# A wait on the run-sum fourteen visits back before every second gather of a graph kernel

## The reference

```python
def _L0_gnn_ref(x, W, M, edge_src, edge_dst):
    self_term = x @ W
    msg = x @ M
    agg = jax.ops.segment_sum(msg[edge_src], edge_dst, num_segments=x.shape[0])
    return jax.nn.relu(self_term + agg)
...
x = x + _L0_gnn_ref(_layernorm(x, axis=-1), L0_gnn_W, L0_gnn_M, src, dst)
x = x + _L0_ffn_ref(_layernorm(x, axis=-1)[None], ...)[0]
```

## Time and profile before

| | |
|---|---|
| median of 3 runs | 4304.4 us |
| their range | 4269.7 to 4313.66 us |
| profiled execution, first to last instruction | 4291.8 us |
| first gather of the first graph to the start of its last run-sum | 63.7 to 2811.1 us |
| median gather of the visits | 946 ns |

### The profile page before, as it was taken

One profiled execution on the slowest core, in us unless ns is written; L12 is line 12 of the kernel. 1 busy time (PEld: TensorE's weight loads), 2 busy tenths in 40 slices (PEclk: granted clock), 3 DMA queues, 4 the chain that ended last, 5 costly groups with the idle time before them and its releaser, 6 DMA issues. The chain is left out here.

```text
span 4291.8 us, 43359 instructions
## 1 busy us (share of the span) xinstructions
PE 2685.8 (63%) x13459; PEld 2000.5 (47%) x13459; DVE 2156.3 (50%) x5820; ACT 902.7 (21%) x1563; POOL 2161.1 (50%) x2248
## 2 busy tenths in 40 slices
PE   2465766676665676766777766761197555556754
PEld 1343544454443444554555544541196444445653
DVE  5676666666644444544444444420045444445666
ACT  3001111111122222111111111110054333334433
POOL 4565665556554565554555555557502434343121
PEclk9667988887887888888888888885598777777877
DMA  9575665655555565555555655540131111111146
GB/s 288 168 239 170 199 186 160 189 170 184 176 175 157 176 186 168 163 184 165 181 183 174 186 182 183 186 97 11 13 105 33 32 35 33 25 43 34 43 129 191
DMA packets 476804, 601.22 MB, mean 140 GB/s; under 512 B 72486, under 2 KB 415390, under 8 KB 474526
## 3 DMA queue, kind: packets, MB, share of 16 engines
q1 hardware_dynamic: 378766, 375.94, 26.7%
q0 software_dynamic: 97216, 219.88, 18.9%
q10 hardware_dynamic: 592, 2.64, 0.2%
HBM read 313.06 MB, written 286.79 MB: 140 GB/s over the span
## 5 line engine op out<-in xcount | busy, mean ns | idle before, releaser
L1700 POOL DMA_INDIRECT ring<-xn_d,srci x1611 | 1564.8, 971 | 1165.6 <-issue 453.7
L1504 PE MATMUL wide<-ring,one_hot 128*128 128x256 f32 x3222 | 984.0, 441 | 631.1 <-DVE ring L817 460.0
L817 DVE SCALAR_TENSOR_TENSOR ring<-ring,same_v,wide 128x256 f32<-128x256 f32 x1610 | 769.8, 478 | 1193.4 <-remote 662.5
L1504 PEld LDWEIGHTS wide<-ring,one_hot 128*128 128x128 f32 x3222 | 665.9, 218 | 900.3 <-issue 489.9
L1610 PE MATMUL wide<-tab_parts,low_hot 128*128 128x208 bf16 x6288 | 656.5, 261 | 334.1 <-issue 312.7
L1734 POOL DMA_INDIRECT g<-tab_d,srt x500 | 479.1, 958 | 633.3 <-DMA sum_d<-g 484.3
L1610 PEld LDWEIGHTS wide<-tab_parts,low_hot 128*128 128x128 bf16 x6288 | 575.6, 100 | 415.2 <-issue 380.3
L1562 PE MATMUL wide<-w2s,hh 128*128 128x256 f32 x1568 | 428.1, 422 | 149.6 <-issue 89.4
L1552 PE MATMUL wide<-xt,w1s 128*128 128x512 f32 (+1 forms) x832 | 423.4, 637 | 41.5 <-ACT hh L1237 39.4
L1237 ACT ACTIVATE hh<-wide,b1c 128x512 f32<-128x512 f32 (+1 forms) x208 | 137.7, 662 | 1469.0 <-remote 584.8
L1562 PEld LDWEIGHTS wide<-w2s,hh 128*128 128x128 f32 x1568 | 337.9, 217 | 225.7 <-issue 103.3
(11 more groups left out here) (369 smaller groups left out, 1740.9 us busy)
## 6 DMA issues: line engine op xcount, KB each, us to landing
run_d<-ring SPq DMA_DIRECT2D x201, 1024.0 KB
ring<-xn_d,srci POOLq DMA_INDIRECT x1611
y_d<-yo SPq DMA_DIRECT2D x196, 128.0 KB
comb<-y_d SPq DMA_DIRECT2D x28, 896.0 KB, 10.5
low_row<-low_d SPq DMA_DIRECT2D x13, 1024.0 KB
sum_d<-g SPq DMA_DIRECT2D x15, 768.0 KB, 3.4
g<-tab_d,srt POOLq DMA_INDIRECT x500
xn_d<-ring SPq DMA_DIRECT2D x7, 896.0 KB, 6.9
```

The lines of the kernel that those rows point to most:

```text
L817: dve_at["run", j] = step(V.scalar_tensor_tensor(out=o, in0=ring[:, (j - 1) // JC % RING, (j - 1) % JC, :], scalar=same_v[:, j:j + 1], in1 ...
L1504: T.matmul(wide[:, 4 + j // 2 % 2, j % 2 * D:(j % 2 + 1) * D], one_hot[:, j // 4 % 4, j % 4, :], ring[:, j // JC % RING, j % JC, :], start ...
L1700: G.indirect_dma_start(out=ring[:, s, j % JC, :], out_offset=None, in_=xn_d, in_offset=at_rows(srci[:, j:j + 1])).then_inc(sem(f"gather{s} ...
```

## The change

Before every gather of an even visit from the fourteenth on, GpSimd waits until VectorE has made the run-sum of the visit fourteen places back. The new constant shifts the line numbers by one up to the place of the wait, and by three behind it.

```diff
@@ -28,6 +28,7 @@
 LATE = 2
 EARLY_STARTS = 27
+LEAD = 14
 
@@ -1697,6 +1698,8 @@
                 G.wait_ge(dve_step, dve_at["run", (c - RING + 1) * JC])
             for j in range(c * JC, c * JC + size(c)):
+                if j % 2 == 0 and j >= LEAD:
+                    G.wait_ge(dve_step, dve_at["run", j - LEAD])
                 G.indirect_dma_start(out=ring[:, s, j % JC, :], out_offset=None, in_=xn_d,
                                      in_offset=at_rows(srci[:, j:j + 1])).then_inc(sem(f"gather{s}"), 16)
```

## The result

The changed kernel takes **4020.7 us** in the median of four runs (4014.0 to 4036.9), the kernel before 4301.2 us beside it (four runs, 4269.7 to 4313.7): a ratio of **0.936, 95% interval 0.932 to 0.941**. The forecast was 4140 us. The direction and the range came out, and the mechanism in part; the gain is 6.4% where 3.8% was forecast.

A forecast was written before the change was run, and what follows sets the result against it. Waiting was taken to bound the kernel, notably VectorE's 662.5 us of "remote" waits while gather rows held TensorE. Holds -172, clock -30 and smaller lead +40 made -162 us: 4140 us forecast, 3.8% less, range 3900 to 4400 us.

The forecast's parts named there:

- Some microseconds into an unbroken row of gathers TensorE's work stops coming through: Visits and late stage: TensorE's work is held beside gathers, from 8 to 10 us into a row in the visits.
- It comes back only some microseconds after the row ends: Visits: TensorE's held work resumes 1.45 to 2.95 us after GpSimd's last gather of the row, say 2.2 us.
- Its own cost: GpSimd's queue in the visits: the added wait costs nothing where the run-sum is done; bounds 0 and 8 us.
- How long a hold lasts: VectorE's "remote" waits before run-sums: about 3.5 us each instead of 5.4, since GpSimd stops sooner.
- How many holds: VectorE's "remote" waits before run-sums: 140 instead of 123, 490 us in all, a gain of 172 us.
- The clock: TensorE in the visits: shorter holds leave less time at lower granted clock, a gain of 30 us, bounds 0 and 170.
- the smaller lead: Chunk heads in the visits: TensorE may wait for late-landing gathers, a cost of about 40 us, bounds 0 and 261.
- slower: Rival: landings at chunk heads stop TensorE with no gain from holds, about 4500 us, from 4350 up; chance 0.21.
- The sum: Whole kernel: -172 - 30 + 40 = -162 us against the profiled span of 4291.8 us.
- Nearly vanish: Rival: short idles between pairs of gathers remove four fifths of the 662 us of holds, about 3830 us; chance 0.17.
- No change: Rival: holds are proportional to the gathers and merely cut smaller, or the wait never decides, 4304 us; chance 0.17.

## Why the prediction was right, and where it was off

**"Some microseconds into an unbroken row of gathers TensorE's work stops coming through".** Shown for the chips of 4300 us: without the gathers the remote waits go from 662.5 us to none, and GpSimd busy with something else, in shorter rows, does not bring them back. Not a rule of the chip type: on two others a row of 160 holds nobody.

**"It comes back only some microseconds after the row ends".** Half right. Both holds that I had looked at ended so, but 59 of the 123, 270.2 us, ended within a row, and the longest was one of them.

**"Its own cost: nothing."** Right on those chips: with the wait before every gather, twice as many waits, the ratio is 0.933.

**"How long a hold lasts", 3.5 us.** It became 4.0 in the mean and 8.4 at the longest where 6 was forecast. The step was nearly right; the release after GpSimd stopped took 1.98 us in the hold shown and 1.9 in the median of the 81 that ended after their row, where 2.2 was taken.

**"How many holds", 140.** This is the term that was mis-sized. I argued that they would become more, since GpSimd pauses less at the ring; there were 102. So the holds saved 256.6 us and not 172. The prediction saw the new wait only as a stop inside a hold. For the holds that end after their row that is what came: 17 more, as I had added, and shorter by 1.7 us in the mean where I took 1.9, but together only 36.5 us less. The other 220 us are in the holds that ended within a row, which the prediction did not know of. With the new wait the visits' gathers run in 223 rows of 7.2 in the mean where they ran in 137 of 11.8, so it also cuts rows that would have grown into a hold; the wait at the chunk heads, which stops GpSimd but leaves rows as long as before, has 115 holds of 5.8 us and wins nothing. That the forecast came as near as it did is in part luck: a saving put down to one kind of hold was mostly made in the other. What separates the two effects cleanly, pauses without any tie to the run-sums, met a chip without holds and stays untried.

**"The clock", 30 us, and "the smaller lead", 40 us.** The clock rose by 0.03 and 0.05, and matmuls waited 76 us for gathers where under 60 was expected (their weight loads, which the prediction did not count, 164.7 us). In the account of VectorE they meet in one line, the wait for the visits' matmuls, 333.3 us before and 326.0 now: together they cost nothing where +10 us were forecast. At 14 the landing is not always covered: weight loads waited for one 59 times, where one chunk in seven, 29, was taken. But a lead of 20 leaves 19.1 us of matmuls' waits for gathers and is no faster, so this costs next to nothing. At 10 it does cost, and 1.9% slower is the "slower" rival's mechanism in full.

**The sum.** -256.6 (holds), -7.3 (clock and landing together) and +11 (issue) make -253 of the 268 us between the two spans.

**The rivals.** "Nearly vanish" is possible only at a price: with a lead of 10 the holds are 34.5 us. "No change" said that TensorE's work is held in proportion to the gathers, however they are grouped; the same 1611 gathers make 662.5 us of holds or 34.5, so that was wrong. Nor did its other ground hold on these chips, that no row of gathers could hold TensorE; on the two other chips none did. "Slower" by landings is what the pairs do there, by about 1.2%.

What the prediction could not see is that 4304 us is a time of some chips. It took the 662.5 us as the kernel's and not as the chip's.

## What to carry to other kernels

Where VectorE's waits end with nothing that the profile can name, look at what another engine was in the middle of, and at all such waits and not at two: here about half of them ended within some 4 us behind a row of GpSimd's gathers and the others within one. If taking the gathers out removes them, cut the rows by waits on the consumer's progress, every second gather rather than every eighth, count how long the rows then really are, and choose the lead by a run on each side: at 14 and 20 visits nothing was lost, at 10 the landings cost more than all holds. And time the kernel before on several chips first: such pacing won 6 to 9% where rows held TensorE and cost 1 to 2% where they did not.

## What the runs showed of the hardware that was not expected

- **Chips differ by 30% on one and the same kernel**: 4357 and 4288 us on two, 3002 and 2997 us on two others. On the first, TensorE trickles in rows of gathers (16 matmuls in 50 us, an expert unit in 33 us); on the others a row of 200 us leaves it 87 to 90% busy. The four chips of the sets were met once each, so a property of the chip and a condition that it was in at that time are not told apart, and what differs no row tells. The transfers do not seem to: the software queue's packets take 18.9% of a span of 4291.8 us (811 us) on one and 25.8% of 3012.7 (777 us) on the other.
- The mean granted clock follows: 0.80 of the whole run with the holds, 0.86 with the first graph's gathers left out, and 0.92 on the chips without holds.
- Beside a GpSimd that reads and writes its memory in rows of some 5 us, VectorE's one-hot tiles take 402 ns in the mean in place of 299, with the median still at 281, and the run-sums stay at 479.
